# State space layers: norm, rounding difference, input scale and residual spread over ScalarE, GpSimd and TensorE; last attention's values copied before they are squared

## The reference

```python
N_LAYERS, D_STATE, EXPAND, D_CONV = 4, 16, 2, 4
def _mamba(x, in_w, cw, cb, xp_w, dt_w, dt_b, A_log, Dp, out_w):
    x_in, z = split(x @ in_w.T)                       # 256 and 256 channels
    xc = silu(causal_conv(x_in, cw) + cb)
    dtr, Bm, Cm = split(xc @ xp_w.T)                  # 8, 16, 16
    dt = softplus(dtr @ dt_w.T + dt_b);  A = -exp(A_log)
    def step(h, inp):                                 # over the 256 positions
        h = h * exp(dt_t[..., None] * A) + (dt_t * u_t)[..., None] * B_t[:, None, :]
        return h, einsum('bdn,bn->bd', h, C_t)
    y = (scan(step) + xc * Dp) * silu(z)
    return y @ out_w.T
...                                                   # each layer: x = x + _mamba(_layernorm(x))
```

## Time and the profile before

| | |
|---|---|
| median of 3 runs | 3192.42 us (3189.2 to 3193.14) |
| profiled execution, its own time | 3191.79 us |
| its span | 3190.1 us |
| PE / DVE / ACT / POOL busy | 2564.0 / 2181.7 / 1629.0 / 1294.9 us |
| scans L1188 | 256 of 2274 ns, 579.7 us, starting from 564.3 to 1587.6 us |
| products with C L1229 | 256 of 2467 ns, 628.7 us |
| decays L1292 | 1024 of 461 ns, 423.5 us |

### The profile page before, as it was taken

How to read it: one execution, slowest core, us unless ns; L and a number is a source line. 1 busy time by engine, 2 the same in 40 slices (tenths; PEclk the granted TensorE clock), 3 DMA queues, 4 the chain that set the end, 5 groups by cost and what they waited for, 6 DMA issues and landing times. The chain is left out here.

```text
span 3190.1 us, 39065 instructions
## 1 busy us (share of the span) xinstructions
PE 2564.0 (80%) x11192; PEld 1537.4 (48%) x11192; DVE 2181.7 (68%) x4403; ACT 1629.0 (51%) x3425; POOL 1294.9 (41%) x1080
## 2 busy tenths in 40 slices
PE   7999785778787777878768999588699967888875
PEld 5767432334344444444323344356444444676764
DVE  6888555999999999999945444466344365445435
ACT  4555332677777676767622344477434323544432
POOL 1000102788888888888800000222100052444344
PEclk9999897899999899989989999799899967888867
DMA  2000222333333333333242211000021100000000
GB/s 96 1 1 0 75 62 72 115 132 133 133 132 131 123 133 133 129 126 131 106 140 54 106 54 53 1 1 0 25 82 53 58 19 1 1 1 0 0 1 13
DMA packets 35666, 209.57 MB, mean 66 GB/s; under 512 B 4032, under 2 KB 5184, under 8 KB 14016
## 3 DMA queue, kind: packets, MB, share of 16 engines
q1 hardware_dynamic: 35520, 207.89, 18.5%
HBM read 205.25 MB, written 2.62 MB: 65 GB/s over the span
## 5 line engine op out<-in xcount | busy, mean ns | idle before, releaser
L1229 POOL TENSOR_TENSOR mam_state_c<-mam_state,weights_r 128x1024 f32<-128x1024 f32 x256 | 628.7, 2467 | 152.2 <-DVE mam_state L1188 152.0
L1360 PE MATMUL banks<-mam_state_c,identity 128*128 128x512 f32 x1024 | 522.8, 640 | 95.5 <-POOL mam_state_c L1229 95.5
L1188 DVE TENSOR_TENSOR_SCAN mam_state<-banks,mam_dbu 128x1024 f32<-128x1024 f32 x256 | 579.7, 2274 | 7.7 <-ACT banks L1292 7.7
L1292 ACT ACTIVATE banks<-mam_dt,mam_a_neg 128x255 f32<-128x255 f32 x1024 | 423.5, 461 | 135.8 <-DVE mam_state L1188 134.5
L1360 PEld LDWEIGHTS banks<-mam_state_c,identity 128*128 128x128 f32 x1024 | 195.8, 204 | 360.2 <-issue 200.5
L1159 DVE TENSOR_TENSOR mam_dbu<-banks,weights_r 128x1024 f32<-128x1024 f32 x192 | 228.2, 1203 | 3.8
L2192 POOL TENSOR_TENSOR at_attention<-at_relu 128x512 f32<-128x512 f32 x128 | 131.7, 1042 | 230.1 <-ACT at_relu L2244 138.6
L424 ACT ACTIVATE at_probs<-banks,at_nmax 128x256 f32<-128x256 f32 x256 | 118.0, 473 | 139.3 <-DVE at_nmax L365 139.3
L2369 PEld LDWEIGHTS banks<-at_v,at_attention 128*128 128x128 f32 x1024 | 161.3, 233 | 33.8 <-issue 29.4
L862 DVE TENSOR_TENSOR m2b_hidden<-m2b_gelu,m2b_comb_spread 128x512 f32<-128x512 f32 x128 | 86.0, 690 | 130.1 <-ACT m2b_gelu L889 119.4
L862 DVE TENSOR_TENSOR m2a_hidden<-m2a_gelu,m2a_comb_spread 128x512 f32<-128x512 f32 x128 | 86.0, 689 | 129.5 <-ACT m2a_gelu L889 119.1
(11 more groups left out here) (478 smaller groups left out, 5342.3 us busy)
## 6 DMA issues: line engine op xcount, KB each, us to landing
weights_r<-mam_bc_rows SPq DMA_DIRECT2D x128, 1024.0 KB, 4.6
m2a_comb_spread<-m2a_comb_rows SPq DMA_DIRECT2D x16, 1024.0 KB, 7.6
m2b_comb_spread<-m2b_comb_rows SPq DMA_DIRECT2D x16, 1024.0 KB, 7.8
m1a_comb_spread<-m1a_comb_rows SPq DMA_DIRECT2D x16, 512.0 KB, 7.9
m1b_comb_spread<-m1b_comb_rows SPq DMA_DIRECT2D x16, 512.0 KB, 8.1
weights_r<-in_mb SPq DMA_DIRECT2D x1, 4332.0 KB, 12.7
weights_r<-in_m SPq DMA_DIRECT2D x1, 4200.0 KB, 13.9
weights_r<-in_a SPq DMA_DIRECT2D x1, 2632.0 KB, 11.5
```

Of the source, the lines that this page charges most:

```text
L1188: dve.tensor_tensor_scan(flat2(h[:, i % 4, :, :, :]), decay(i), flat2(dbu[:, i % 4, :, :, :]), 0.0, ALU.mult, ALU.add).then_inc(h_ready, 1)
L1229: pool.tensor_tensor(hc[:, j % 4, :, :, :], h[:, j % 4, :, :, :], c_rows(j), ALU.mult).then_inc(hc_ready, 1)
L1292: i = act.activation(decay(j)[:, o + 1:o + S], dt[:, q, c, 1:S], ACT.Exp, scale=aneg[:, l, k:k + 1])
L1360: k = pe.matmul(y_bank(q)[:, :], K.ident[:, :], flat(hc[:, j % 4, n, :, :]), start=(j == 0 and n == 0), stop=(j == NP - 1 and n == 1))
```

## The change

In the state space layers:

- The norm is applied by ScalarE in slot 4, behind the decays of pair 5, as Identity with a scale 1/std and a bias -mean/std. GpSimd makes the bias in slot 3 in two small instructions (`mam_ln_bias`).
- The rounding difference is split. ScalarE makes (1 + e) - 1 by a second Identity, behind L1264 and ahead of the Ln, into the tile of |v|. GpSimd subtracts e at the head of its slot 4, ahead of the product with C of pair 3. VectorE keeps only the max and subtraction.
- `input_scale` moves from VectorE (a product of two SBUF tiles) to ScalarE (a Copy of `mam_dt_u` into bank 6), ahead of the next unit's first decays.
- The residual is added by TensorE, which multiplies the residual by an identity into the y bank ahead of each half of the output product; ScalarE copies the bank to `mam_xm` in slot 4.
- `BY_POOL` goes from (3, 6) to (4,): GpSimd makes one input term of a unit, VectorE seven.

In the last attention, GpSimd's 1/sqrt goes to slot 0, ahead of the square of head 0; the application is a scalar_tensor_tensor with the reciprocal broadcast; and VectorE copies a value bank as soon as the product is there, ScalarE then squares the copy.

```diff
-    BY_POOL = (3, 6)
+    BY_POOL = (4,)
...
                     if nxt and i == 4:
                         b = nxt[1] + nxt[0] * B
-                        link = chain(dve, dve_s)
-                        dve.wait_ge(part_ready, b + 1)
-                        link(dve.scalar_tensor_tensor(vw[:, :, :], vu[:, :, :], -1.0, ve[:, :, :], ALU.add, ALU.subtract))
+                        dve.wait_ge(rounding_ready, b + 1)
...
-                    if after and i == 4:
-                        dve.wait_ge(N.rstd, a + 1)
-                        for t in range(TS):
-                            k = dve.scalar_tensor_tensor(N.out[:, t * P:(t + 1) * P], xs(t), N.mv[:, t, 0:1],
-                                                         N.rs[:, t:t + 1].broadcast_to([P, P]),
-                                                         ALU.subtract, ALU.mult)
-                        k.then_inc(N.xn, 1)
...
+                def rounding(i, nxt):
+                    if nxt and i == 4:
+                        b = nxt[1] + nxt[0] * B
+                        pool.wait_ge(part_ready, b + 1)
+                        pool.tensor_tensor(vw[:, :, :], va[:, :, :], ve[:, :, :], ALU.subtract).then_inc(rounding_ready, 1)
+
                 def prepare(i, nxt, after):
                     if after and i == 3:
-                        norm_pool(K, N, pool, after[1] + after[0] * B)
...
+                        pool.tensor_scalar(nb[:, :], N.mv[:, :, 0], -1.0, None, ALU.mult).then_inc(mean_ready, 1)
+                        pool.tensor_scalar(N.rs[:, :], N.mv[:, :, 1], EPS, None, ALU.add).then_inc(N.pool, 1)
+                        pool.wait_ge(N.pool, 2 * (a + 1))
+                        pool.tensor_tensor(N.rs[:, :], N.rs[:, :], K.neg_half[:, 0:TS], ALU.pow).then_inc(N.rstd, 1)
...
+                        pool.tensor_tensor(nb[:, :], nb[:, :], N.rs[:, :], ALU.mult).then_inc(bias_ready, 1)
...
-                        act.activation(vu[:, :, :], ve[:, :, :], ACT.Identity, bias=K.ones[:, 0:1]).then_inc(part_ready, 1)
-                        act.wait_ge(part_ready, b + 1)
+                        act.activation(vu[:, :, :], ve[:, :, :], ACT.Identity, bias=K.ones[:, 0:1]).then_inc(plus_ready, 1)
+                        act.wait_ge(plus_ready, b + 1)
+                        act.activation(va[:, :, :], vu[:, :, :], ACT.Identity, bias=K.neg_one[:, 0:1]).then_inc(part_ready, 1)
                         act.activation(vl[:, :, :], vu[:, :, :], ACT.Ln).then_inc(ln_ready, 1)
...
+                    if after and i == 4:
+                        act.wait_ge(bias_ready, a + 1)
+                        if nxt:
+                            act.wait_ge(N.xt, a)
+                        for t in range(TS):
+                            k = act.activation(N.out[:, t * P:(t + 1) * P], xm[:, bass.ds(s * W + t * P, P)], ACT.Identity,
+                                               bias=nb[:, t:t + 1], scale=N.rs[:, t:t + 1])
+                        k.then_inc(N.xn, 1)
...
+                def input_scale(u, q):
+                    act.wait_ge(dus_ready, u + 1)
+                    if not (isinstance(u, int) and u == 0):
+                        act.wait_ge(dbu_dve, u * (NP - len(BY_POOL)))
+                    act.activation(K.ps[6][:, :], flat(du[:, q, :, :]), ACT.Copy).then_inc(dup_ready, 1)
...
+                        act.activation(xm[:, bass.ds(s * W, W)], y_bank(q)[:, 0:W], ACT.Copy).then_inc(done, 1)
...
                         for t in range(TS):
+                            pe.matmul(y_bank(q)[:, t * P:(t + 1) * P], K.ident[:, :],
+                                      xm[:, bass.ds(s * W + t * P, P)], start=True, stop=False)
...
                         n = i - 5
                         j, c = n // 2, n % 2
+                        dve.wait_ge(v_ps, s * 4 + n + 1)
+                        dve.tensor_copy(v[:, q, j, c * 512:(c + 1) * 512], K.ps[v_bank[n]][:, :]).then_inc(v_sb, 1)
                         dve.wait_ge(v_sq, s * 4 + n + 1)
-                        dve.tensor_copy(v[:, q, j, c * 512:(c + 1) * 512], K.ps[v_bank[n]][:, :]).then_inc(v_sb, 1)
...
-                    if nxt and i == 1:
+                    if nxt and i == 0:
                         norm_pool(K, N, pool, nxt[0])
```

More of the change, by code:

```diff
@@ L1046, in state_space_layers @@
     L, NS, KC, C = m["L"], m["NS"], m["KC"], m["C"]
-    (xm, aneg, skip, xpad, xc, zs, dt, du, rows, va, ve, vl, vu, vw, dbu, h, hc, yg, spread) = (
-        m[n] for n in "xm aneg skip xpad xc zs dt du rows va ve vl vu vw dbu h hc yg spread".split())
+    (xm, aneg, skip, xpad, xc, zs, dt, du, rows, va, ve, vl, vu, vw, dbu, h, hc, yg, nb, spread) = (
+        m[n] for n in "xm aneg skip xpad xc zs dt du rows va ve vl vu vw dbu h hc yg nb spread".split())
     NP = NS // 2
-    BY_POOL = (3, 6)
+    BY_POOL = (4,)
     flat = lambda a: a.rearrange("p c t -> p (c t)")
@@ L1120, in _ @@
                 dve.sem_inc(h_ready, 2)
-                dve.sem_inc(done, 2)
                 def prepare(i, nxt, after):
-                    if after and i in (2, 4):
+                    if after and i == 2:
                         l, s, q = after
@@ L1127, in prepare @@
                         xs = lambda t: xm[:, bass.ds(s * W + t * P, P)]
-                    if after and i == 2:
                         link = chain(dve, dve_s)
+                        if nxt:
+                            dve.wait_ge(bias_ready, a)
                         if l > 0:
@@ L1190, in slot @@
                         if nxt and i + 1 == NP:
[L1191 removed]
                             input_term(u + 1, 0)
[L1193 to L1197 removed]
                     prepare(i, nxt, after)
                 before_units(prepare)
[L1201 removed]
                 input_term(0, 0)
[L1203 removed]
+                over_units(dve, slot, 3)
             @block.gpsimd
             def _(pool):
+                def rounding(i, nxt):
[3 more added lines that the diff above has]
+                        pool.tensor_tensor(vw[:, :, :], va[:, :, :], ve[:, :, :], ALU.subtract).then_inc(rounding_ready, 1)
                 def prepare(i, nxt, after):
                     if after and i == 3:
[L1209 removed]
+                        if nxt:
+                            pool.wait_ge(N.xn, after[1] + after[0] * B)
+                        a = after[1] + after[0] * B
+                        pool.wait_ge(N.stats, a + 1)
+                        pool.sem_inc(N.pool, 1)
+                        pool.tensor_scalar(nb[:, :], N.mv[:, :, 0], -1.0, None, ALU.mult).then_inc(mean_ready, 1)
+                        pool.tensor_scalar(N.rs[:, :], N.mv[:, :, 1], EPS, None, ALU.add).then_inc(N.pool, 1)
+                        pool.wait_ge(N.pool, 2 * (a + 1))
+                        pool.tensor_tensor(N.rs[:, :], N.rs[:, :], K.neg_half[:, 0:TS], ALU.pow).then_inc(N.rstd, 1)
+                        pool.wait_ge(mean_ready, a + 1)
+                        pool.wait_ge(N.rstd, a + 1)
+                        pool.tensor_tensor(nb[:, :], nb[:, :], N.rs[:, :], ALU.mult).then_inc(bias_ready, 1)
                     if nxt and i == 5:
@@ L1241, in slot, with prepare_all @@
                     prepare(i, nxt, after)
-                before_units(prepare)
+                def prepare_all(i, nxt, after):
+                    rounding(i, nxt)
+                    prepare(i, nxt, after)
+                before_units(prepare_all)
                 over_units(pool, slot, 1)
@@ L1303, in slot @@
                             act.wait_ge(dt_ready, u + 2)
+                            input_scale(u + 1, 1 - q)
                             decays(nxt[0], u + 1, 1 - q, 0)
+                    if last and i == 4:
+                        l, s, q = last
+                        act.wait_ge(out_ps, s + l * B + 1)
+                        act.activation(xm[:, bass.ds(s * W, W)], y_bank(q)[:, 0:W], ACT.Copy).then_inc(done, 1)
                     prepare(i, nxt, after)
+                act.sem_inc(done, 2)
                 before_units(prepare)
                 act.wait_ge(dt_ready, 1)
+                input_scale(0, 0)
                 decays(0, 0, 0, 0)
-                over_units(act, slot, 0)
+                over_units(act, slot, 5)
             @block.tensor
@@ L2097, in prepare @@
                     if i == 1:
-                        norm_apply(N, dve, xs, s)
+                        dve.wait_ge(N.rstd, s + 1)
+                        if not (isinstance(s, int) and s == 0):
+                            dve.wait_ge(N.xt, s)
+                        for j in range(TS):
+                            k = dve.scalar_tensor_tensor(N.out[:, j * P:(j + 1) * P], xs(j), N.mv[:, j, 0:1],
+                                                         N.rs[:, j:j + 1].broadcast_to([P, P]),
+                                                         ALU.subtract, ALU.mult)
+                        k.then_inc(N.xn, 1)
                     if i == 2:
```

28 lines of the change are left out of this document (9 added, 19 removed).

## The result

The change takes 3106.03 us (median of 4 runs, 3101.51 to 3107.15), the kernel before 3191.34 us beside it; the ratio is 0.973, 95% interval 0.9713 to 0.9747. That is 85 us less, where 111 us less was predicted.

A forecast was written before the change was run, and what follows sets the result against it. The prediction took VectorE to bound the layers and, after the change, a 29.3 us dependency loop plus 0.8 for TensorE's clock. 3191.8 - 77 (layers) - 34 (last attention) = 3081 us, range 3000 to 3155.

The forecast's parts named there:

- the forecast: Whole kernel: units of 29.3 to 30.9 us in the layers, 3042 to 3110 us in all, chance 0.61.
- VectorE's program: Layers: VectorE's own instructions lose 6.29 us and gain 1.11 a unit, so alone it would need 27.4 us.
- the ring: Layers: dependency loop from scan 5 to next scan 2, |v|, ScalarE's decays and scan 5 again; 29.3 us a unit.
- a rival for the change itself: Layers: VectorE stays the bound and no loop through other engines binds; 2995 us, chance 0.13.
- What is late next: Layers: ScalarE's decays for pair 5 come 9.1 us after |v|, so VectorE stalls before scan 5, some 2 us.
- The second Identity: Layers: ScalarE's added instruction for the split difference, 0.71 us, delays pair 5's decays from 8.34 to 9.1 after |v|.
- The clock: Layers: TensorE's gap of about 3.7 us before pair 3's sum lowers its clock; 1.6 us more in half the units.
- 30.9 us in every unit: Layers: unit length if the gap brings TensorE's half clock back in all units, by the Trainium skill's rule.
- Layers, 77 us: State space layers: units fall from 32.55 to 30.1 us, times 31.5 units; bounds 20 to 163 us.
- Last attention, 34 us: Last attention: 24 us from TensorE's waits for the norm plus 10 us from its clock staying up.
- The norm edit: Last attention: reciprocal in slot 0 lets the application start earlier, gaining 3.5 of 3.80 us, x 7 = 24 us.
- The values' order: Last attention: copying before squaring makes VectorE wait one square, covered by idle time; counted zero, bounded by 19 us either way.

The follow-up runs named there:

- dt_norm: The change with TensorE's dt product at the head of its slot 2 and GpSimd's norm bias behind pair 3's product with C (slot 4): 3037.85 us, ratio 0.9512.
- vector_difference: The change with the rounding difference back on VectorE, without ScalarE's second Identity and GpSimd's difference: 3071.83 us, ratio 0.9615.
- dt_first: The change with TensorE's dt product at the head of its slot 2, ahead of the sum, skip and output products: 3077.48 us, ratio 0.9614.
- rounding_behind: The change with GpSimd's difference behind its product with C of pair 3 instead of ahead of it: 3103.69 us, ratio 0.9699.
- dt_norm_values: The change with the dt product first in slot 2, GpSimd's norm bias in slot 4, and the attention values' old order (square, then copy): 3018.08 us, ratio 0.9451.
- sums_later: The change with VectorE's sum of the squared values one slot behind the copy in the last attention: 3066.54 us, ratio 0.9603.

## Why the prediction was right, and where its numbers were off

The time lies in the range and the forecast was the case that came: the units take 29.9 us on the average, between the 29.3 and 30.9 that it named. 25 us lie between the predicted time and the measured one. The time of that case, 3042 to 3110 us, was added up wrongly at its upper end: with 30.9 us a unit and the 10 us that it gave the attention at least, it is 3191.8 - 52 - 10 = 3130.

- **VectorE's program.** Predicted at 27.4 us a unit; with the ring open (dt_norm) units are 27.66, busy 791.51 of 800, that is 27.4. Right. VectorE stayed the bound only there, in the two runs that add to dt_norm and in vector_difference; as a rival for the change itself it was wrong, as the 72.5 us of waits show.
- **What is late next.** The stall stands where it was forecast, ahead of scan 5, at 1.86 us, and the links of the ring measure 2.96, 9.14 and 17.2 against the predicted 3.05, 9.1 and 17.1. dt_first, which shortens only the first link, takes that stall away: the ring is shown.
- **The second Identity.** The forecast counted it with 0.71 us in the ring, but not that dropping it is worth more than the whole gain of moving the difference. The change's split took 1.8 us from VectorE and paid it with 0.7 in the ring and 1.3 in TensorE's gap; by vector_difference that trade costs 37 us.
- **The clock.** Forecast: a gap of some 3.7 us ahead of pair 3's sum, slow in half of the units, 1.6 us more there. Measured: gaps of 3.30 to 3.50 us, the clock down behind each of 29, and 1.1 us more in the 15 units whose whole sum is slow. So the half was right by luck: the clock falls everywhere, and a unit is longer only where it comes back late. The extra wait stands ahead of scan 1 and not in the ring's own TensorE part. That the clock makes the unit longer is borne out by dt_first, where behind the same gap of 3.31 us a unit takes 27.57 with the sum at 1.98 and 28.78 to 30.58 with a slow one, and by rounding_behind, where a shorter gap leaves 5 long units of 29. The Trainium skill (TensorE: Matmul & The Clock Gate, Why this matters for your kernels) has gaps bring half clock back; the change's trace agrees in all 29 units. What the prediction made of it, 30.9 us in every unit, did not come.
- **Layers, 77 us.** Measured 69. From first to last scan they lost 1023.3 - 948.5 = 74.8; the rest went ahead of the first scan, which comes 4.7 us later. Of the rows, the first pair is before, the second with the change:

```profile
553.85 0.66 PE L152 MATMUL banks<-identity,mam_ln_xn 128*128 128x128 f32 x2 [5.45 <-DVE mam_ln_xn L1148]
...
556.01 3.89 PE L1346 MATMUL banks<-mam_xn_padded,weights_r 128*128 128x256 f32 x16
```
```profile
556.43 0.66 PE L152 MATMUL banks<-identity,mam_ln_xn 128*128 128x128 f32 x2 [6.94 <-ACT mam_ln_xn L1276]
...
558.60 5.49 PE L1368 MATMUL banks<-mam_xn_padded,weights_r 128*128 128x256 f32 x16
```

  ScalarE applies the norm behind the second Identity and the Ln, so the transposes come 2.6 us later; the convolution's products behind them take 1.6 us more; and behind these stands ScalarE's input scale of 0.6, ahead of the first decays. Together that is 4.7. L1142's wait there, 17.3 of its 18.1 us, is not the cause: nothing on the way to the convolution stands behind it now. The prediction had no term for the work before the first unit.
- **Last attention, 34 us.** Measured 17. The norm edit did what was said: no wait ahead of the transposes in the loop. It is worth 48 us by the ratios and 29 by the spans, where 24 and 10 for the clock were predicted; the values' order took some of it back, so the 17 is the difference of two larger numbers. **The step that failed is "The values' order ... I count it at zero, bounded by ... 19 us either way".** It costs 18 us by the spans, 19 in the pair dt_norm and dt_norm_values, 31 by the first ratios: at or beyond the bound. The argument was that idle time covers VectorE's wait for a square, since it is busy for half of the stage. VectorE is idle on the average, but four copies and four sums stand in front of a relu that TensorE waits for; the wait of 0.70 comes four times, and where it is gone (sums_later) so is the loss. Why 2.8 us of waits a sequence cost 41 / 7 = 5.9 us is in part the clock: in sums_later the sequences at a granted clock of 1.00 take 40.1 us and one at 0.88 takes 43.9, while the change's shortest, at 0.89, takes 47.0. At a like clock the waits would then be worth some 3 us, an estimate from these three; no run parts the two.

## What to carry to other kernels

Work moved off a full engine is worth no more than the distance to the next ring: write down the ring through the other engines, and ask of each added instruction whether it stands in it. Here one Identity of 0.7 us and one small difference stood in it, and keeping them on the full engine was faster. When two causes hold a loop (a late link and a gap that lowers the clock), the edits alone can show little (37 and 4 us) and both together much (70); try them together before either is dropped. And an idle share of a stage covers a wait only if nobody waits for what stands behind it on the same queue.

## What the runs showed of the hardware

- The same gap ahead of the same sum lowers the clock in one pass of the loop and not in the next. The sum takes 1.98 us with the clock up and 3.78 when it is down from end to end. It was slow, in part or whole, in all 29 passes of the change (gaps of 3.30 to 3.50 us), in 25 of 29 of dt_first (3.31 to 3.32), in 13 of 29 of rounding_behind (2.07 to 2.12), in 11 of 29 of vector_difference (2.07 to 2.11) and in none of 29 of dt_norm (1.55 to 1.62).
- An attention sequence whose granted clock is 1.00 takes 40.1 us; those of the kernel before took 50.6 to 52.5 at 0.77 to 0.83.
- Two 512-column tiles of SBUF cost VectorE 1.61 us as a median here beside a busy GpSimd, 0.69 at best, and GpSimd 1.26 in either place.
